# Moving the sums, divisions and turned logits to the end of a score step in an attention and expert kernel

## The reference

```
x = x + tanh(g_xattn) * xattn(layernorm(x), ctx)
x = x + tanh(g_ffn) * ffn(layernorm(x))

xattn(x, y): q = x Wq + bq; k = y Wk + bk; v = y Wv + bv    (16 heads of 16)
             attn = softmax(q k^T / 4); out = attn v
             relu(out W1 + b1) W2 + b2
ffn(x):      shared expert(x) + sum over the top 2 of 8 experts, by sigmoid(x Wr + rb),
             of score * expert(x);  expert(x) = (silu(x Wg) * (x Wu)) Wd
```

## Time and profile before

| what | value |
|---|---|
| median of 3 runs | 1178.47 us |
| the profiled execution's own time | 1180.16 us |
| its span, first to last instruction | 1178.4 us |
| TensorE matmul (PE) busy | 1095.5 us, 93% |
| TensorE weight load (PEld) busy | 534.8 us, 45% |
| VectorE (DVE) busy | 657.3 us, 56% |
| ScalarE (ACT) busy | 570.7 us, 48% |
| GpSimd (POOL) busy | 136.2 us, 12% |

### The profile page before, as it was taken

One profiled execution on the slowest core, in us unless ns is written; L12 is line 12 of the kernel. 1 busy time (PEld: TensorE's weight loads), 2 busy tenths in 40 slices (PEclk: granted clock), 3 DMA queues, 4 the chain that ended last, 5 costly groups with the idle time before them and its releaser, 6 DMA issues. The chain is left out here.

```text
span 1178.4 us, 15206 instructions
## 1 busy us (share of the span) xinstructions
PE 1095.5 (93%) x5534; PEld 534.8 (45%) x5534; DVE 657.3 (56%) x895; ACT 570.7 (48%) x1056; POOL 136.2 (12%) x156
## 2 busy tenths in 40 slices
PE   4879999999999999999999999978869999999983
PEld 2433335434434433534433433435536666666652
DVE  4598776886676787677797685103412222222245
ACT  2107776776676776567777577623111111111110
POOL 4500000020000002000000003200550000000055
PEclk9859999999999999999999999859989999999998
DMA  9753505531505532505333501005820111111125
GB/s 314 114 93 38 60 1 61 102 46 16 61 1 60 96 39 30 61 1 60 38 41 45 59 3 59 5 5 174 321 94 18 45 45 45 46 45 45 36 72 151
DMA packets 51129, 78.08 MB, mean 66 GB/s; under 512 B 10993, under 2 KB 36210, under 8 KB 51058
## 3 DMA queue, kind: packets, MB, share of 16 engines
q1 hardware_dynamic: 45184, 66.87, 29.9%
q0 software_dynamic: 3072, 8.39, 2.2%
q10 hardware_dynamic: 2802, 1.85, 0.6%
HBM read 32.34 MB, written 16.52 MB: 41 GB/s over the span
## 5 line engine op out<-in xcount | busy, mean ns | idle before, releaser
L521 ACT ACTIVATE probs<-ring_ps 128x512 f32<-128x512 f32 (+1 forms) x832 | 443.4, 597 | 184.4 <-PE ring_ps L651 179.9
L755 DVE TENSOR_REDUCE mpart<-s_ps 128x2 f32<-128x1024 f32 x384 | 457.9, 1219 | 100.4 <-PE s_ps L638 98.9
L651 PE MATMUL ring_ps<-qst,kst 64*128 64x512 f32 (+1 forms) x832 | 233.8, 471 | 3.7 <-ACT probs L521 3.1
L666 PE MATMUL pv_ps<-probs,vp 128*32 128x512 f32 (+2 forms) x1664 | 226.2, 617 | 0.7 <-ACT probs L521 0.7
L638 PE MATMUL s_ps<-kst,qst 63*128 63x512 f32 (+1 forms) x1024 | 194.2, 419 | 11.8 <-DVE mpart L755 11.6
L651 PEld LDWEIGHTS ring_ps<-qst,kst 64*128 64x128 f32 (+1 forms) x832 | 102.4, 183 | 216.5 <-ACT probs L521 98.8
L962 ACT ACTIVATE s_sb<-gu_ps 128x512 f32<-128x512 f32 x55 | 32.8, 597 | 277.6 <-PE gu_ps L1039 277.6
L1039 PE MATMUL gu_ps<-wgu,xbT 128*128 x312 | 140.3, 593 | 0.0
L638 PEld LDWEIGHTS s_ps<-kst,qst 63*128 63x128 f32 x1024 | 95.6, 194 | 90.6 <-DVE mpart L755 68.9
L1168 DVE TENSOR_TENSOR h_sb<-s_sb,gu_ps 128x512 f32<-128x512 f32 x55 | 37.8, 687 | 174.8 <-ACT s_sb L962 174.8
L430 POOL COPY rspread<-rden 128x512 f32<-128x512 f32 x16 | 9.8, 612 | 674.6 <-DVE rden L798 674.6
(11 more groups left out here) (128 smaller groups left out, 712.2 us busy)
## 6 DMA issues: line engine op xcount, KB each, us to landing
kst<-parts SPq DMA_DIRECT2D x64, 200.5 KB, 4.4
kst<-parts SPq DMA_DIRECT2D x64, 100.2 KB, 4.2
sorted_x<-zeros SPq DMA_DIRECT2D x1, 4992.0 KB, 19.7
xb<-sorted_x SPq DMA_DIRECT2D x39, 128.0 KB, 2.2
sorted_y<-ysb SPq DMA_DIRECT2D x39, 128.0 KB, 1.7
qst<-parts SPq DMA_DIRECT2D x64, 64.0 KB, 4.2
wgu<-in_WgT SPq DMA_DIRECT2D x16, 256.0 KB, 7.9
wgu<-in_WuT SPq DMA_DIRECT2D x16, 256.0 KB, 8.1
```

The source lines that it names most:

```text
L521: nc.scalar.activation(probs[0:w, m % NPB, h, :], ring_ps[0:w, bank(("st", idx)), :], ACT.Exp, scale=SCALE).then_inc(exp_done, 1)
L651: nc.tensor.matmul(ring_ps[0:w, bank(("st", idx)), :], kst[u % NKB][rows, h // 2, mt * P:mt * P + w], qst[u % NKB][rows, h // 2, :], start ...
L666: last = nc.tensor.matmul(pv_ps[32 * h:32 * h + c1 - c0, :], values[:, c0:c1], probs[0:w, m % NPB, h, :], start=(mt == 0), stop=(mt == MT ...
L755: nc.vector.tensor_reduce(mpart[:, heads, t, q], s_ps[:, n % NSP], AX.X, ALU.max).then_inc(s_free, 1)
```

## The change

```diff
+LAST_IN_STEP = ("SUM", "DIV", "XT2", "LG")
@@ the ring's order
-        ring += [("st", idx) for idx in (4 * m - 1, 4 * m) if idx >= 0] + jobs + [("st", 4 * m + 1), ("st", 4 * m + 2)]
+        ring += [("st", idx) for idx in (4 * m - 1, 4 * m) if idx >= 0]
+        ring += [job for job in jobs if job[0] not in LAST_IN_STEP] + [("st", 4 * m + 1), ("st", 4 * m + 2)]
+        ring += [job for job in jobs if job[0] in LAST_IN_STEP]
@@ TensorE
                 for job in jobs:
-                    do(job)
+                    if job[0] not in LAST_IN_STEP:
+                        do(job)
                 for pair in chunk[1:2]:
                     score(pair)
                 st(at + 1)
                 st(at + 2)
+                for job in jobs:
+                    if job[0] in LAST_IN_STEP:
+                        do(job)
                 if at > 0:
                     pv(MT * u + mt - 1)
```

## The result

The changed kernel takes 1194.71 us, the median of four runs (1193.58 to 1196.02), against 1177.70 for the kernel before, also of four (1173.60 to 1181.26). The ratio is 1.0146, 95% interval 1.011 to 1.0182: slower by some 17 us. Slower was forecast, but 1186.7, and the range ended at 1193. The profiled execution took 1195.31, its span 1193.6 (1178.4 before).

A forecast was written before the change was run, and what follows sets the result against it. It took the step to be bound by a 2.60 us latency loop through ACT and TensorE. +3.9 (28 steps) and +4.3 (unit 15) gave +8.2 on the profiled 1180.16, 1188.4; less 1.7 to the median, 1186.7 us, range 1180.5 to 1193.

The forecast's parts named there:

- The loop: Step without a job: latency loop through ACT and TensorE (exponential, release, `st`, `pv`, `st` to ACT), 2.60 us.
- the place in the ring: Job between the scores takes one bank, so `st(4m+2)` waits for the second exponential: 0.49 us, job's own time hidden.
- The wait charged to DVE: Weight-load waits on `on`, 14 times 0.84, 11.7 us (`rden` as much): not to be had, since `pv` streams then.
- 28 steps, +3.9: `SUM` and `DIV` steps, units 1 to 14: 3.23 against 3.09 us, +0.14 each; sum +3.9, from -1.4 to +6.2.
- Rival 1: Job cheaper ahead of `pv`, 0.44 for four transposes: the 28 steps stay near 3.05 to 3.09; 1181.5 us, chance 0.19.
- rival 2: Faster: 0.49 goes in 38 steps, the job hidden behind the third and fourth exponential; 19 less, 1160 us, chance 0.06.
- DVE costs nothing: Job's reader behind the second maximum: next step's first maximum covered by 0.19 us, multiply just in time; cost nothing.
- Unit 15, +4.3, "between 2.5, all at the high clock, and 8, if more steps fall low": Last unit, no score pairs: moved `DIV`, `LG`, `XT2`, `SUM` and the last step lengthen, some at low clock; +4.3 us.
- Rival 3, the clock: Clock stays low from unit 15's `SUM` on: some seven steps more cost about 1 us each; near 1194, chance 0.08.
- The experts' part keeps its length: Experts start after the last step, nothing of theirs loaded earlier in another way; the shift goes through to the end.
- The price by the Trainium skill: Moved job at 4 x 0.081 = 0.32 us, step 2.97: 28 steps gain 3.4, total about unchanged; the trace disagreed.

The follow-up runs named there:

- e3: Changed kernel with `DIV` making one of its four transposes: the 14 `DIV` steps 2.93 us against 3.25; total 1191.98 us, one run.
- e4: Kernel before (old order) with `DIV` making one of its four transposes: `DIV` steps stayed at 3.09 us, one run.
- e9: Changed kernel with the moved jobs placed behind `pv` in place of ahead of it: 1190.35 us, one run.
- e10: Kernel before with `MX` alone moved between `st(4m-1)` and `st(4m)`, ring accordingly: ratio 0.9962 to the kernel before.
- e5: Changed kernel with two pairs of unread matmuls added in each step without score pairs: ratio 1.0046 to the kernel before.
- e11: Kernel before with two pairs of unread matmuls added in each step without score pairs, except those with `LG`: ratio 0.9957 to the kernel before.

## Why the prediction was wrong

- *The loop*, 2.60 as exponential, `st`, `pv`, `st`: right. e3, e4 and e9 show both sides of it: a job between the scores hides its own time, and one in the loop costs its own time. That it is the place in the ring that costs, e10 bears out: `MX` dealt another place made its step 0.31 shorter.
- *The wait charged to DVE is not real*: right. It vanished by name and not by length.
- *28 steps, +3.9*: measured 28 x 0.163 = 4.6. I had 0.05 + 0.58 on a step of 2.60, the trace 0.06 + 0.59. Rival 1, a cheaper job ahead of `pv`, fell, and so did rival 2, with steps of 2.60.
- *DVE costs nothing*: right with four transposes (0.00 a step); e3 shows how near it was.
- *Unit 15, +4.3, "between 2.5, all at the high clock, and 8, if more steps fall low"*: this is the step that failed. Measured 9.9 in the first profile and 12.5 in the second (59.6 against 47.1). The order's own share was about right: over the ten steps from `SUM` on that e5 and e11 both ran at the full clock, the changed order costs 2.8, and the forecast's terms at the high clock give 2.6 for them. Two things failed, both on the low clock. The first is the price of a low step: I took the new order at 5.0, close to the 5.10 and 5.11 measured, but subtracted 4.54, the old order with the whole step at the low clock. No `SUM` or `XT2` step of the kernel before is that long: the longest took 4.03 (the step of the earlier trace rows) and 4.06 (`SUM`), since the clock was low in a part of them only. So these two gained 1.08 and 1.04 where I had 0.45 and 0.4. The second is that I kept the clock pattern of the kernel before, with two `XT2` steps and one `SUM` step as low. By kind of step:

| steps of unit 15 | before, us | now, us | change | forecast |
|---|---|---|---|---|
| `SUM` | 4.06 | 5.10 | +1.04 | +0.4 |
| the plain step behind it | 2.59 | 3.45 | +0.86 | 0 |
| `DIV` | 3.08 | 3.25 | +0.17 | +0.14 |
| `XT2`, five steps | 17.32 | 20.87 | +3.55 | +1.3 |
| `LG`, two steps | 7.46 | 10.05 | +2.59 | +1.6 |
| the last step | 6.71 | 8.39 | +1.68 | +0.85 |

  In the last step the matmuls of `LG` alone took 3.45 in place of 1.92: before, the clock was back up when they ran.
- *Rival 3, the clock*, named the mechanism, its place and 1194, and got a chance of 0.08. The earlier trace rows showed the clock falling already while TensorE was nearly full; I should have given more weight to a change that empties these steps further keeping it down longer. Its 1194 is within 1 us of the median, in part by luck: the clock did not stay low from `SUM` on but went up and down (1.00 at 750 to 760), and the 7 us that it adds to the forecast stand against 5.6 more in unit 15, 0.7 more in the 28 steps and a start 0.5 later.
- *The experts' part keeps its length*: right in the two profiles (397.7 and 397.7 behind the last `pv`), although over all profiles it varies from 393.5 to 397.8 with nothing changed there.
- *The price by the Trainium skill* ("TensorE: Matmul & The Clock Gate", "Back-to-back issue gap", about 81 ns): such a job would have left the steps under 3.09. The runs disagree: they have 0.33 for three transposes more, 110 ns each, and 0.26 for the first.

## What to carry to other kernels

Before moving work out of a stall, close the loop that sets the step and ask for each place whether it lies in it: here moving a job freed a wait of 0.49 and put 0.65 in its stead. Where a ring of buffers is dealt out in program order, a job's cost can be the slot it takes and not its time, and a job of hardly any length shows which (`MX`, 3.10). And where the clock already drops in a stretch, price every lengthened step there at the low clock first.

## What the runs showed of the hardware

- Work that nobody reads made the kernel faster: 26 pairs of 63x512 matmuls in unit 15 and the three steps ahead, with the jobs in the old order (e11), held the granted clock at 1.00 from 720 to 770 us, where the kernel before had 0.83 to 1.00 and the changed one 0.66 to 1.00, and saved 5 of the 47 us of unit 15.
- The same program runs unit 15 in 57.0 or 59.6 us with the low clock in other places: two profiles of one kernel can differ by 2.6 us in a stretch of 57.
- The 16 matmuls of `LG`, 1.95 us in the other steps, stretched to 3.45 in the last step of the changed kernel, where the granted clock fell to 0.50 (790 to 800). In the second profile they took 3.55 there.

```profile
789.28 3.45 PE L611 MATMUL ring_ps<-wr,parts 128*128 128x8 f32 x16 [0.88 <-DVE parts L787]
```
